# Delta output projection, last layer norm and ternary feed-forward joined in one stage over tiles

## What is computed

```python
# end of the delta attention: out is its output, gate a sigmoid gate
out = out * gate
mu = jnp.mean(out, axis=-1, keepdims=True)
var = jnp.mean(jnp.square(out - mu), axis=-1, keepdims=True)
out = (out - mu) * jax.lax.rsqrt(var + 1e-05) * norm_w
h = h + out @ Wo
# ternary feed-forward
x = _layernorm(h)
scale = jnp.maximum(jnp.mean(jnp.abs(w)), 1e-08)         # of W1 and of W2
w_t = jnp.clip(jnp.round(w / scale), -1.0, 1.0)
y = gelu(x @ w_t1.T + b1) @ w_t2.T + b2
h = h + y
```

## Time and profile before

| | |
|---|---|
| median of three runs | 2141.74 us |
| lowest, highest | 2136.63, 2148.51 us |
| the profiled execution's own time | 2141.01 us |
| its span, first to last instruction | 2139.2 us |
| busy in the span: PE | 1671.6 us (78%) |
| DVE | 1319.8 us (62%) |
| ACT | 709.8 us (33%) |
| POOL | 443.3 us (21%) |
| mean granted TensorE clock | 0.868 of full speed |

### The profile page before, as it was taken

One profiled execution on the slowest core, in us unless ns is written; L12 is line 12 of the kernel. 1 busy time (PEld: TensorE's weight loads), 2 busy tenths in 40 slices (PEclk: granted clock), 3 DMA queues, 4 the chain that ended last, 5 costly groups with the idle time before them and its releaser, 6 DMA issues. The chain is left out here.

```text
span 2139.2 us, 34723 instructions
## 1 busy us (share of the span) xinstructions
PE 1671.6 (78%) x13217; PEld 1493.3 (70%) x13217; DVE 1319.8 (62%) x3135; ACT 709.8 (33%) x1332; POOL 443.3 (21%) x592
## 2 busy tenths in 40 slices
PE   5677777599999999899999997880780780843689
PEld 5476666289999999799999995770770770742468
DVE  3745555655555556546464656569569669677885
ACT  2344443222232323223232323550450450431232
POOL 0323221000000000000000002427227337354450
PEclk9789897689999999999999997995895985975589
DMA  3100000110101010101010101000000000001001
GB/s 134 48 2 1 0 0 2 41 40 1 40 1 40 1 40 1 41 1 40 1 40 1 40 1 34 1 1 0 1 0 0 0 0 0 1 1 42 1 1 47
DMA packets 10408, 36.91 MB, mean 17 GB/s; under 512 B 3208, under 2 KB 6176, under 8 KB 7456
## 3 DMA queue, kind: packets, MB, share of 16 engines
q1 hardware_dynamic: 10272, 35.14, 4.7%
HBM read 32.64 MB, written 2.49 MB: 16 GB/s over the span
## 5 line engine op out<-in xcount | busy, mean ns | idle before, releaser
L850 ACT ACTIVATE hidden<-bank,moe_b 128x512 f32<-128x512 f32 (+1 forms) x320 | 213.3, 668 | 531.0 <-PE bank L807 531.0
L824 PE MATMUL bank<-moe_w2h,hidden_lo 128*128 128x256 f32 x1216 | 344.1, 283 | 0.0
L824 PE MATMUL bank<-moe_w2l,hidden_hi 128*128 128x256 f32 x1216 | 344.1, 283 | 0.0
L824 PE MATMUL bank<-moe_w2h,hidden_hi 128*128 128x256 f32 x1216 | 343.9, 283 | 0.0
L864 DVE SCALAR_TENSOR_TENSOR residual<-bank,gates,residual 128x256 f32<-128x256 f32 x152 | 73.5, 484 | 289.5 <-PE bank L824 289.5
L807 PE MATMUL bank<-x_hi,moe_w1h 128*128 128x512 f32 (+1 forms) x640 | 244.2, 382 | 7.8 <-issue 6.4
L807 PE MATMUL bank<-x_lo,moe_w1h 128*128 128x512 f32 (+1 forms) x640 | 243.7, 381 | 0.0
L807 PE MATMUL bank<-x_hi,moe_w1l 128*128 128x512 f32 (+1 forms) x640 | 243.3, 380 | 0.0
L824 PEld LDWEIGHTS bank<-moe_w2l,hidden_hi 128*128 128x128 f32 x1216 | 233.3, 192 | 1.2
L824 PEld LDWEIGHTS bank<-moe_w2h,hidden_hi 128*128 128x128 f32 x1216 | 233.2, 192 | 1.2
L824 PEld LDWEIGHTS bank<-moe_w2h,hidden_lo 128*128 128x128 f32 x1216 | 233.3, 192 | 0.0
(11 more groups left out here) (266 smaller groups left out, 3574.1 us busy)
## 6 DMA issues: line engine op xcount, KB each, us to landing
moe_w<-in_moe_w SPq DMA_DIRECT2D x18, 1024.0 KB, 5.0
patches<-in_patches SPq DMA_DIRECT2D x8, 864.0 KB, 4.5
out<-residual SPq DMA_DIRECT2D x19, 128.0 KB, 1.7
ffn_w<-in_ffn_w SPq DMA_DIRECT2D x2, 1024.0 KB, 6.0
att_w<-in_att_w SPq DMA_DIRECT2D x1, 1536.0 KB, 5.9
delta_w<-in_delta_w SPq DMA_DIRECT2D x1, 1280.0 KB, 5.8
tok_w<-in_tok_w SPq DMA_DIRECT2D x1, 768.0 KB, 4.1
delta_wvf<-in_delta_wvf SPq DMA_DIRECT2D x1, 272.0 KB, 5.7
```

Source lines behind the costliest of these rows:

```text
L824: mm = nc.tensor.matmul(bank[4 + n % 4][:, 0:D], left, right, start=(i == 0), stop=(i == len(passes) - 1))
L850: nc.scalar.activation(H[:, i % 4, 0:n], bank[i % 4][:, 0:n], ACT.Relu, bias=b1[:, group * TOGETHER + x, f:f + 1]).then_inc(acted, 1)
```

## The change

It has three parts.

- Both ternary weights are made by POOL in stage "lno" (six instructions in a row, each over 128x2048; is_lt now ahead of is_gt), none in "delta_o".
- Stages "delta_o", "ln3" and the feed-forward become one stage. A class `ResidualTurn` holds one tile's steps, and each engine has a loop over j = 0 to 21 (22 on DVE) ahead of its feed-forward work. PE: the product of tile j, then the transposes of tile j-3. DVE: add j, low part j-4, statistics j, reciprocal j-1, aggregate j. ACT: square root j (one column, the epsilon as bias), then the high part j-3. PE's `hidden(0)` waits for the low part of all tiles.
- The tile is normalised by POOL, not by DVE, in this stage; the square root and the reciprocal are taken for each tile by itself. POOL's bias additions come after its 19 normalisations. The products rotate over three banks, the transposes over three others.

```diff
-            layer_norm_turn(nc, bank, Y, STD, MV, XN, XH, XL, ident, "lno", pool_work=ternary(0))
-            add_product_and_stats(nc, bank, RES, BN, MV, XH, XL, wh[:, O], wl[:, O], "delta_o", pool_work=ternary(1))
-        layer_norm_turn(nc, bank, RES, STD, MV, XN, XH, XL, ident, "ln3")
-        ternary_ffn(nc, sb, bank, RES, XH, XL, out, w1t, w2t, b1, b2)
+            def ternary(pool, done):
+                for i in range(2):
+                    nc.gpsimd.tensor_scalar(down[:], flat[i], S[:, 3, i:i + 1], None, ALU.is_lt).then_inc(done, 1)
                     nc.gpsimd.tensor_scalar(up[:], flat[i], S[:, 2, i:i + 1], None, ALU.is_gt).then_inc(done, 1)
+                    pool.wait_ge(done, 3 * i + 2)
                     nc.gpsimd.tensor_tensor(tern[i], up[:], down[:], ALU.subtract).then_inc(done, 1)
+                    pool.wait_ge(done, 3 * i + 3)
+
+            layer_norm_turn(nc, bank, Y, STD, MV, XN, XH, XL, ident, "lno", pool_work=ternary)
+        ternary_ffn(nc, sb, bank, RES, BN, MV, STD, XN, XH, XL, ident, wh[:, O], wl[:, O], out, w1t, w2t, b1, b2)
...
+    def multiply(self, pe, t):
+        ring = len(self.product_banks)
+        if t >= ring:
+            pe.wait_ge(self.summed, t - ring + 1)
...
+    def turn(self, pe, t):
+        ring = len(self.turn_banks)
+        pe.wait_ge(self.normed, t + 1)
+        if t >= ring:
+            pe.wait_ge(self.lo_ready, t - ring + 1)
...
+    def deviation(self, act, t):
+        act.wait_ge(self.mv_ready, t + 1)
+        self.nc.scalar.activation(self.STD[:, 1, t:t + 1], self.MV[:, t, 1:2], ACT.Sqrt,
+                                  bias=self.eps[:, 0:1]).then_inc(self.std_ready, 1)
...
+    def normalise(self, pool, t):
+        pool.wait_ge(self.inv_ready, t + 1)
+        if t >= 4:
+            pool.wait_ge(self.turned, t - 3)
+        self.nc.gpsimd.tensor_scalar(self.XN[:, t % 4, :], self.RES[:, t, :], self.MV[:, t, 0:1],
+                                     self.STD[:, 2, t:t + 1], ALU.subtract, ALU.mult).then_inc(self.normed, 1)
...
             def _(pe):
...
+                for j in range(TILES + LAG):
+                    if j < TILES:
+                        line.multiply(pe, j)
+                    if j >= LAG:
+                        line.turn(pe, j - LAG)
+                pe.wait_ge(x_lo, TILES)
...
             def _(act):
+                act.wait_ge(eps_set, 1)
+                for j in range(TILES + LAG):
+                    if j < TILES:
+                        line.deviation(act, j)
+                    if j >= LAG:
+                        line.high(act, j - LAG)
...
             def _(dve):
...
+                nc.vector.memset(eps[:], EPS).then_inc(eps_set, 1)
+                for j in range(TILES + LAG + 1):
+                    if j < TILES:
+                        line.add(dve, j)
+                    if 0 <= j - LAG - 1 < TILES:
+                        line.low(dve, j - LAG - 1)
+                    if j < TILES:
+                        line.stats(dve, j)
+                    if 0 <= j - 1 < TILES:
+                        line.invert(dve, j - 1)
+                    if j < TILES:
+                        line.aggregate(dve, j)
...
             def _(pool):
                 for t in range(TILES):
+                    line.normalise(pool, t)
+                for t in range(TILES):
+                    pool.wait_ge(normed, t + 1)
                     nc.gpsimd.tensor_tensor(RES[:, t, :], RES[:, t, :], b2[:, :], ALU.add).then_inc(biased, 1)
```

More of the change, by code:

```diff
@@ L186, in add_product_and_stats @@
+TURN_SEMAPHORES = ("product", "sum", "bn", "mv", "std", "inv", "normed", "turned", "x_hi", "x_lo")
 def add_product_and_stats(nc, bank, RES, BN, MV, OH, OL, wh, wl, name, pool_work=None):
@@ L1180, in _ @@
                             nc.vector.bn_aggr(MV[:, t - 2, :], BN[:, t - 2, :]).then_inc(mv_ready, 1)
-            def ternary(i):
-                def work(pool, done):
+            def ternary(pool, done):
+                for i in range(2):
+                    nc.gpsimd.tensor_scalar(down[:], flat[i], S[:, 3, i:i + 1], None, ALU.is_lt).then_inc(done, 1)
                     nc.gpsimd.tensor_scalar(up[:], flat[i], S[:, 2, i:i + 1], None, ALU.is_gt).then_inc(done, 1)
-                    nc.gpsimd.tensor_scalar(down[:], flat[i], S[:, 3, i:i + 1], None, ALU.is_lt).then_inc(done, 1)
-                    pool.wait_ge(done, 2)
+                    pool.wait_ge(done, 3 * i + 2)
                     nc.gpsimd.tensor_tensor(tern[i], up[:], down[:], ALU.subtract).then_inc(done, 1)
-                return work
-            layer_norm_turn(nc, bank, Y, STD, MV, XN, XH, XL, ident, "lno", pool_work=ternary(0))
-            add_product_and_stats(nc, bank, RES, BN, MV, XH, XL, wh[:, O], wl[:, O], "delta_o", pool_work=ternary(1))
-        layer_norm_turn(nc, bank, RES, STD, MV, XN, XH, XL, ident, "ln3")
-        ternary_ffn(nc, sb, bank, RES, XH, XL, out, w1t, w2t, b1, b2)
+                    pool.wait_ge(done, 3 * i + 3)
+            layer_norm_turn(nc, bank, Y, STD, MV, XN, XH, XL, ident, "lno", pool_work=ternary)
+        ternary_ffn(nc, sb, bank, RES, BN, MV, STD, XN, XH, XL, ident, wh[:, O], wl[:, O], out, w1t, w2t, b1, b2)
 def chunk_buffers(sb, ctx, i):
@@ L1794, in _, with ternary_ffn @@
                                             ALU.add).then_inc(pool_solved, 1)
-def ternary_ffn(nc, sb, bank, RES, XH, XL, out, w1t, w2t, b1, b2):
+def ternary_ffn(nc, sb, bank, RES, BN, MV, STD, XN, XH, XL, ident, woh, wol, out, w1t, w2t, b1, b2):
     with ExitStack() as ctx:
@@ L1802, in ternary_ffn @@
         HL = sb(ctx, "fhidden_lo", [P, 2, FB, MT * P], F32R)
+        eps = sb(ctx, "eps", [P, 1])
+        LAG = ResidualTurn.LAG
         steps = [range(t, min(t + MT, TILES)) for t in range(0, TILES, MT)]
-        with stage(nc, "f_up", "f_act", "f_hi", "f_lo", "f_down", "f_bias", "f_out", "stored") as (
-                block, up_ready, acted, h_hi, h_lo, down_ready, biased, out_ready, stored):
+        with stage(nc, *("do_" + n for n in TURN_SEMAPHORES), "f_eps",
+                   "f_up", "f_act", "f_hi", "f_lo", "f_down", "f_bias", "f_out", "stored") as (
+                block, product, summed, x_bn, x_mv, std_ready, inv_ready, normed, turned, x_hi, x_lo, eps_set,
+                up_ready, acted, h_hi, h_lo, down_ready, biased, out_ready, stored):
+            line = ResidualTurn(nc, bank, RES, BN, MV, STD, XN, XH, XL, ident, woh, wol, eps, (4, 5, 6), (0, 1, 2),
+                                product, summed, x_bn, x_mv, std_ready, inv_ready, normed, turned, x_hi, x_lo)
             @block.tensor
```

49 lines of the change are left out of this document (added).

## The result

The changed kernel takes 2153.91 us (median of 20 runs, 2144.69 to 2164.84) against 2141.34 us for the kernel before (20 runs, 2135.13 to 2156.49). The ratio is 1.0053 with a 95% interval of 1.0034 to 1.0072: slower by half a per cent, as forecast (2155.0 us, 0.65%).

The account below looks back on a forecast made before the run. The last-ending chain ran through the feed-forward only; barriers made "lno", "delta_o" and "ln3" count at full length, DVE's normalisations held by POOL mattering most. 2141.0 + 13.6 + 1.7 - 1.3 gave 2155.0 us, 8-in-10 range 2145 to 2162.

Parts of the forecast that it names:

- Step 1: In "lno", POOL's six ternary instructions would hold six DVE normalisations instead of three: +13.6 us.
- Step 1's second half: In "delta_o", taking the ternary work out would give nothing back, as POOL there ran beside DVE.
- Step 2: From first delta product to first hidden block, joining the stages would take 34.8 us against 33.10: +1.7 us.
- The loop: In the joined stage, aggregate to next aggregate through ACT's square root and high part, then DVE: 1.63 us a tile.
- the drain: End of the joined stage, after the last add starts: finishing the remaining tiles, 5.05 to 5.3 us.
- Step 3: At the feed-forward's start, earlier bias additions and an earlier DVE start would save time: -1.3 us.
- the biases: At the feed-forward's start, POOL's bias additions ending earlier would make 0.8 cast and low-part pairs cheaper: -0.8 us.
- PE at the higher level: At the feed-forward's start, a higher PE clock level would let DVE start up to 0.9 us earlier: -0.5 us.
- A: In "lno", POOL's second three instructions would not hold DVE: +3.3 us there, 2144.7 us in all; chance 0.12.
- B: In the joined stage, POOL's normalisation would set the pace; at 2.0 us each, 2164.4 us; chance 0.07.
- C: In the joined stage, the path through ACT would be shorter, DVE ruling: -6 us, 2149 us; chance 0.10.
- D: In the joined stage, 33 us of two passes would shrink to some 20 us: 2140.3 us; chance 0.05.

Follow-up runs that it names:

- e1: The kernel before with POOL making both ternary weights in "lno" and none in the delta projection; 2151.47 us, ratio to before 1.0051.
- e5: The changed kernel with each of POOL's six ternary instructions in "lno" cut into four over 512 columns; 2149.79 us (one run).
- e12: The changed kernel with the first weight's comparisons cut: is_lt into 1024 and 1024 columns, is_gt into 1536 and 512; 2158.34 us (one run).
- e2: The changed kernel without the second ternary weight on POOL, ACT copying that weight unrounded instead; 2137.99 us, ratio to before 0.9997.
- e3: The changed kernel with ACT's high part j-3 put ahead of square root j in the joined stage; 2148.53 us, ratio to before 1.0035.
- e4: The changed kernel with POOL normalising only 128 of the 256 columns in the joined stage; 2156.36 us (one run).
- e8: The changed kernel with POOL's bias additions waiting for the last low part before the feed-forward; 2158.93 us (one run).
- e6: The kernel before with the first ternary weight's two comparisons moved from "lno" into the gate stage; 2130.13 us, ratio to before 0.9947.

## Why the prediction was right, and where not

Step 1, both ternary weights in "lno", +13.6 us: measured +13.6 (first projection matmul at 2039.74 in place of 2026.19), and +13.6 alone in e1. The count of held instructions was right, six in place of three, each to the end of its POOL instruction. What stood behind it, that a hold lasts as long as the POOL instruction, is too wide: e5 and e12 show it for subtractions and for comparisons over 1536 and 2048 columns only. The step was safe since it moved instructions of the same size.

Step 1's second half, nothing back in the projection stage: 0.0 in e1.

Step 2, the join, +1.7 us: measured +1.57, and +1.3 in e2. The loop was given as 1.63 us a tile and used as 1.64, though its terms add up to 1.62, and it is 1.60 to 1.61; e3 and e4 show that it is the loop and not POOL. Its terms leave out the reciprocal between statistics and aggregate (0.11 us from start to start) and take the statistics 0.12 too long, which cancels. One term was mis-sized: POOL's normalisation takes 1.22 us, not 0.85. The row over 2048 columns with one operation was scaled down with too small a fixed part and nothing for the second operation; 0.80 us for 128 columns and 1.22 for 256 make it 0.38 us fixed and 3.3 ns a column. It lay within the bounds of 0.68 to 1.53, and under the loop, so the sum saw only the drain. The upper bound of 1.8 us that the text gives for the drain doesn't follow from its terms, which give 0.7.

That step 2 came out within 0.2 us is in part luck, as two errors of about half a microsecond cancel. The last add begins 28.9 us after the first product, not 29.5; and the drain from there takes 5.8 us, not 5.05 to 5.3, of which POOL's longer normalisation is 0.37. That the clock would rise in between was right: 0.50 at first, 1.00 from 2048 to 2072 us, 0.89 over the stage. But it is down again by the drain, where PE is busy 0.69 of 2.40 us and the granted clock is 0.51.

Step 3, the start of the feed-forward, -1.3 us: measured -1.3, and e8 takes it back alone. That the sum fits is luck, as its split into 0.8 for the biases and 0.5 for PE at the higher level was wrong. PE began the hidden blocks at the lower level, first in the kernel before and then in the changed one:

```profile
2059.20:2063.00 3.80, 3.71 (x9) 2.96 (x10) 0.90 (x1) 1.97 (x2) 3.72 (x6) 0.50 0.00 0
```

```profile
2074.40:2078.50 4.10, 4.09 (x10) 3.23 (x11) 1.23 (x2) 1.76 (x3) 4.10 (x7) 0.50 0.00 0
```

DVE's first cast comes 2.8 us after the first hidden matmul in both, so the 0.5 us for PE were nothing. The biases are worth all of it: POOL begins them 1.7 us ahead of the first hidden matmul, six of DVE's low parts are slow beside them in place of seven (a pair 0.97 us cheaper), and the first cast takes 0.58 us in place of 0.94.

The rivals: A fell in the trace (the fourth to sixth L135 are held). B fell, but by 0.4 us a tile and not by more than twofold as the text had it; with ACT's order turned POOL is nearly full, and DVE with it. B's 44.2 us is more than its own terms give: 0.41 us more a tile over 14 to 18 tiles and 1.2 in the drain make 41.7 to 43.4. C and D fell with the pace of 1.60; what D hoped for takes the turned order, and then is 5 us and not 13.

## What to carry to other kernels

Before work is put on POOL, read what DVE does in that stage: its SBUF-to-SBUF tensor_scalar stopped for POOL's long instructions here, and its cast and low part from SBUF were slowed by POOL's additions, while what reads PSUM, statistics and aggregates ran on; an instruction that is held shows as a long busy one, not as a wait. Joining stages with in-order engines makes loops through their orders: write down what stands ahead of each step on its engine, for a two-line turn of the order was worth more (5.4 us) than the two barriers (0.68 us for the one that was read). And where the chain of waits names an engine that itself waits in each turn, halve its work in an experiment before it is believed.

## What the runs showed of the hardware

- POOL's comparison over 512 columns holds DVE's normalisation by 0.04 us where it is issued 0.42 us after the comparison's start, and to the comparison's end where it is issued in its last half microsecond (0.22 us); over 1024 columns two got through in the middle of one; over 1536 and 2048 it holds to its end. A subtraction holds to its end at 512 columns already (1.02 of 1.3 us). The reason is open.
- A DVE tensor_scalar over 19 columns, 0.17 us by itself, is held to the end of POOL's subtraction as one over 256 is: 4.51 us in e6.
- DVE's cast and low part over 512 columns, both from SBUF, and POOL's bias additions slow each other: 0.96 for 0.42 us and 1.11 for 0.69, and POOL needs 1.0 us for an addition beside them and 0.69 alone.
- POOL, tensor_scalar with two operations and two scalars per partition: 0.80 us for 128 columns, 1.22 for 256.
- The executions of one kernel spread by 12 us and more, and much of that lies ahead of the changed stages: the gate stage's first matmul came between 1970.7 (granted clock 0.869 over the span) and 1977.7 us (0.865) in kernels that are alike up to there. A change of 13 us is measured better from a stage's own start than by the median of a few runs.
